# The mean of a group norm: token tiles added on GpSimd ahead of one matmul, with both halves of a convolution moved before it

## What is computed

```python
x = x + L0_conv(_ln_c(x))        # layer norm, in_proj, causal convolution of 4 taps, selective scan over 16 states, projection
t = t + L0_ffn(_ln_t(t))         # tokens; values rounded to fp8 ahead of a 256x256 linear layer
x = x + L1_conv(_ln_c(x))        # group norm with 32 groups, then attention over channels:
    # mean = jnp.mean(xg, axis=(2, 3, 4)); var = jnp.var(xg, axis=(2, 3, 4))
    # xn = (xg - mean) * rsqrt(var + EPS), then Q, K, V, softmax(Q K^T / 16), output linear layer
t = t + L1_ffn(_ln_t(t))         # mixture of 8 experts, the best 2 for each token
```

## Time and profile before

| what | value |
|---|---|
| median of 3 runs | 1844.05 us (1843.04 to 1844.74) |
| the profiled execution | 1846.15 us |
| its span, first to last instruction | 1844.4 us |
| mean granted TensorE clock | 0.960 |
| PE busy | 1562.0 us (85% of the span) |
| DVE busy | 1182.3 us (64%) |
| POOL busy | 1074.2 us (58%) |
| ACT busy | 946.9 us (51%) |

### The profile page before, as it was taken

One profiled execution on the slowest core, in us unless ns is written; L12 is line 12 of the kernel. 1 busy time (PEld: TensorE's weight loads), 2 busy tenths in 40 slices (PEclk: granted clock), 3 DMA queues, 4 the chain that ended last, 5 costly groups with the idle time before them and its releaser, 6 DMA issues. The chain is left out here.

```text
span 1844.4 us, 22487 instructions
## 1 busy us (share of the span) xinstructions
PE 1562.0 (85%) x6433; PEld 996.5 (54%) x6434; DVE 1182.3 (64%) x1368; ACT 946.9 (51%) x1758; POOL 1074.2 (58%) x574
## 2 busy tenths in 40 slices
PE   5588898988789888888898888773499999999997
PEld 2233335643335553333564333453388888888896
DVE  3399998489998579999658989846622222222222
ACT  6857665876664876775677666431022222222222
POOL 0499991279994159999037999400345555545543
PEclk9899999999999999999998999996699999999999
DMA  3256560156662057564025656552022222222221
GB/s 103 95 204 211 208 214 1 49 190 234 221 214 73 1 168 250 189 213 159 2 74 192 234 194 228 207 215 71 21 34 38 34 38 36 40 34 37 37 31 28
DMA packets 78400, 222.41 MB, mean 121 GB/s; under 512 B 12588, under 2 KB 31349, under 8 KB 74966
## 3 DMA queue, kind: packets, MB, share of 16 engines
q1 hardware_dynamic: 62390, 202.54, 31.6%
q0 software_dynamic: 15904, 18.66, 6.3%
HBM read 199.76 MB, written 19.82 MB: 119 GB/s over the span
## 5 line engine op out<-in xcount | busy, mean ns | idle before, releaser
L462 PE MATMUL psum<-HC_sb,ident_sb 128*128 128x512 f32 x768 | 371.4, 609 | 39.0 <-DVE HC_sb L1561 24.8
L462 PE MATMUL psum<-experts_sb 64*128 64x512 f32 (+5 forms) x882 | 275.3, 548 | 78.6 <-DVE HC_sb L1561 24.3
L1968 ACT ACTIVATE hgt_sb<-psum_moe,b_sb 128x256 f32<-128x256 f32 (+1 forms) x312 | 116.2, 455 | 380.8 <-PE psum_moe L1875 380.8
L1127 ACT ACTIVATE psum<-experts_sb 128x1024 f32<-128x1024 f32 x192 | 212.7, 1111 | 168.3 <-DVE experts_sb L1551 106.9
L1551 DVE TENSOR_TENSOR_SCAN experts_sb<-psum,DBX_sb 128x1024 f32<-128x1024 f32 x108 | 244.2, 2276 | 23.6 <-ACT psum L1127 17.2
L2120 DVE TENSOR_TENSOR YS_sb<-psum_moe,b_sb 128x256 f32<-128x256 f32 x71 | 30.2, 425 | 356.2 <-PE psum_moe L1875 356.2
L1875 PE MATMUL psum_moe<-XGT_sb,w1s_sb 128*128 128x256 f32 (+1 forms) x1248 | 254.1, 362 | 0.0
L1875 PE MATMUL psum_moe<-experts_sb,hgt_sb 128*128 x1136 | 251.7, 379 | 0.7 <-DVE YS_sb L2120 0.7
L1852 POOL DMA_INDIRECT out<-YS_sb,scat_sb x71 | 129.1, 1818 | 207.2 <-DVE YS_sb L2124 192.1
L462 PEld LDWEIGHTS psum<-HC_sb,ident_sb 128*128 128x128 f32 x768 | 139.4, 192 | 199.8 <-issue 101.7
L1875 PEld LDWEIGHTS psum_moe<-XGT_sb,w1s_sb 128*128 128x128 f32 x1248 | 219.0, 191 | 25.3
(11 more groups left out here) (298 smaller groups left out, 2379.4 us busy)
## 6 DMA issues: line engine op xcount, KB each, us to landing
DA_sb<-bc_rows SPq DMA_DIRECT2D x96, 512.0 KB, 4.8
X_XT_sb<-bc_rows SPq DMA_DIRECT2D x92, 512.0 KB, 4.1
experts_sb<-bc_rows SPq DMA_DIRECT2D x48, 512.0 KB, 5.1
SQ_sb<-bc_rows SPq DMA_DIRECT2D x48, 512.0 KB, 5.4
T_sb<-bc_rows SPq DMA_DIRECT2D x20, 512.0 KB, 5.8
experts_sb<-w1T SPq DMA_DIRECT2D x8, 1024.0 KB, 18.5
experts_sb<-w2T SPq DMA_DIRECT2D x8, 1024.0 KB, 20.4
X_sb<-x_tok SPq DMA_DIRECT2D x5, 1024.0 KB, 6.9
```

The source lines that it names most:

```text
L462: return nc.tensor.matmul(o, lhsT, rhs, start=start, stop=stop, **k)
L1127: nc.scalar.activation(DECAY_SB if is_turned(i) else decays[i % 2], DT[:, c, :], ACT.Exp, scale=a_neg[:, s:s + 1]).then_inc(da_ready, 1)
L1968: m = nc.scalar.activation(HGT[:, k, 4 * h + q, 0:w], psum[:, 2 * h + q // 2, (q % 2) * 2 * P:(q % 2) * 2 * P + w], ACT.Gelu, bias=b1[:, b ...
```

## The change

POOL adds the eight normed token tiles of an image into `HSUM`, 256 columns of `SQ`, with seven additions, each of which waits for its tile and for the addition before it (the first also for the end of the fp8 rounding, whose scratch lies there). PE then needs one matmul with `mean_w`. It waits for the seventh addition of the image, and in PE's list the second half of the convolution stands ahead of it. On POOL the additions come first in `between`; for the last image they follow after the loop.

```diff
+        HSUM = SQ[:, 0, HL + C:L]
...
             def group_sum(p):
-                for n in range(NB):
-                    pe.wait_ge(h_done, p * NB + n + 1)
-                    i = mm(psum[:, 0, 0:C], mean_w[:, :], XT[:, n, 0:C], n == 0, n == NB - 1)
-                i.then_inc(gm_ready, 1)
+                pe.wait_ge(token_sum, (p + 1) * (NB - 1))
+                mm(psum[:, 0, 0:C], mean_w[:, :], HSUM, True, True).then_inc(gm_ready, 1)
...
                 if go_on:
                     conv_pair(b, 1, 0)
+                    conv_pair(b, 1, 1)
                 group_sum(p)
-                if go_on:
-                    conv_pair(b, 1, 1)
                 gram(p)
...
+            def sum_tokens(p):
+                for n in range(1, NB):
+                    pool.wait_ge(h_done, p * NB + n + 1)
+                    if n == 1:
+                        pool.wait_ge(q_step, p * 10 + 10)
+                    else:
+                        pool.wait_ge(token_sum, p * (NB - 1) + (n - 1))
+                    nc.gpsimd.tensor_tensor(HSUM, HSUM if n > 1 else XT[:, 0, 0:C], XT[:, n, 0:C], ALU.add).then_inc(token_sum, 1)
+
             def between(b):
+                sum_tokens(b - 1)
                 pool.wait_ge(g_step, b * 5)
...
             with pool.Fori(1, B) as b:
                 between(b)
                 scans(b, True)
+            sum_tokens(B - 1)
```

More of the change, by code:

```diff
@@ L316, in build_front @@
         ff_ready = sem("ff_ready"); x2_done = sem("x2_done")
-        h_done = sem("h_done"); ones_set = sem("ones_set"); gm_ready = sem("gm_ready"); gm_done = sem("gm_done")
+        h_done = sem("h_done"); token_sum = sem("token_sum"); ones_set = sem("ones_set"); gm_ready = sem("gm_ready"); gm_done = sem("gm_done")
         hc_done = sem("hc_done"); gram_ready = sem("gram_ready"); gram_done = sem("gram_done")
```

## The result

The change made the kernel slower: a median of 1848.81 us (1847.70 to 1853.25, 7 runs) against 1843.04 us for the kernel before in the same comparison (1841.79 to 1844.74, 7 runs), a ratio of 1.0034 with a 95% interval of 1.0022 to 1.0045, so +6.3 us (+4.1 to +8.3). The profiled execution took 1849.37 us with a span of 1847.5 and a mean granted clock of 0.952; before it was 1846.15, 1844.4 and 0.960. The change shifted the helper's line from L462 to L464.

A forecast was written before the change was run, and what follows sets the result against it. PE sets the pace in conv stages; the last stage is one chain. Three times -0.2, plus 2.4, 0.5, 1.9 and 3.0, gave +7.2 us: 1851.2 on the 1844.05 median, range 1846.0 to 1855.5.

The forecast's parts named there:

- the leading case: Clock lost in the last stage and in two or three conv stages: 1849.5 to 1855.5 us, chance 0.57.
- the first rival: Clock lost in the last stage and in one conv stage at most: 1848.2 to 1849.8 us, chance 0.25.
- POOL's step: Start to start of POOL's chained adds at the norm: 0.87 us, bounds 0.73 and 0.96.
- The conv stages' term: Gram matrix in each of three conv stages starts 0.2 us earlier; bounds -0.9 to +0.4.
- The last stage's chain: Last stage: POOL's adds delay DVE's start on the mean by 2.4 us; bounds +1.6 and +3.0.
- The mean at half clock: Last stage: the one mean matmul runs at 1.2 GHz and takes twice as long, +0.5 us.
- The gram matrix of the last stage: Last stage: gram matrix at 1.2 GHz for its first 3.8 us, +1.9 us; bounds 0 and 7.2.
- The conv stages' clock: Two of three conv stages lose the full clock at 1.5 us each, +3.0 us; bounds none and three.
- The row before 590: Second stage, old profile: PE ran 1.43 of 3.5 us before 590; the next 3.5 stood at 0.52 clock.
- no clock is lost at all: Rival: full clock kept in all stages, +1.8 us, 1845.9 us, no measurable change; chance 0.14.
- The faster one: Rival: conv stages get back all 3.3 us of PE's work each, -7.5 us in sum, 1836.6 us; chance 0.04.
- the late mean in the last stage: Sign for the prediction: last stage, DVE starts on the mean 2.4 us or more later, counted from ACT's first normed tile.

The follow-up runs named there:

- e3: The whole change plus matmuls with unread results around the mean in the last stage, against the kernel before: 1844.50 us, ratio 1.0002.
- e6: The whole change plus matmuls with unread results after the mean in conv stages and around it in the last, against the kernel before: 1843.65 us, ratio 0.9997.
- e5: POOL's sum and one matmul, but in the old place between the convolution's halves, against the kernel before: 1854.71 us, ratio 1.0057.
- e9: The changed kernel run once more, unaltered, against the kernel before: 1848.24 us, ratio 1.0031.
- e4: Second half of the convolution moved ahead of the mean, which still takes eight matmuls, against the kernel before: 1852.92 us, ratio 1.0054.
- e2: The change in conv stages only, plus four matmuls with unread results behind the mean there, against the kernel before: 1840.92 us, ratio 0.9982.

## Why the prediction was right, and where its steps were not

The time, 1848.81, lies in the range, 2.4 us under the forecast, and the cause is the one that was forecast: POOL's chain in the last stage, and PE's clock where the tiles no longer keep it at work. But it lies below 1849.5, where the range of the leading case began, and inside the 1848.2 to 1849.8 of the first rival, and both traces of the change show that rival's one loss in a conv stage. Most terms of the sum were mis-sized, and their errors partly cancel; that the total came so near is in part luck.

**POOL's step** is the first: 0.87 us was taken. In the conv stage six adds in a row take 4.49 us, with 0.75 from start to start, near the lower bound of 0.73; in the last stage 4.79, with 0.81. POOL's timeline of the changed kernel, the first two of these six in either stage:

```profile
324.38 0.64 POOL L1210 TENSOR_TENSOR SQ_sb<-SQ_sb,X_XT_sb 128x256 f32<-128x256 f32 x1
325.09 0.73 POOL L1210 TENSOR_TENSOR SQ_sb<-SQ_sb,X_XT_sb 128x256 f32<-128x256 f32 x1
...
1206.80 0.64 POOL L1210 TENSOR_TENSOR SQ_sb<-SQ_sb,X_XT_sb 128x256 f32<-128x256 f32 x1
1207.58 0.72 POOL L1210 TENSOR_TENSOR SQ_sb<-SQ_sb,X_XT_sb 128x256 f32<-128x256 f32 x1
```

The adds last 0.64 to 0.73 us instead of 0.731, and the gap between dependent ones is 0.07 us in the conv stage and 0.14, as taken, in the last. From the second tile to the seventh add's end the conv stage took 328.87 - 323.43 = 5.44 us, the last 5.70, where 6.15 had been summed up. The rule of the Trainium skill (Perfetto Trace Analysis, section GPSIMD Engine Instruction) on spacing is borne out again: 0.75 and 0.81 from start to start beside a median span of 0.68.

**The conv stages' term** of -0.2 follows from it and was too small: -0.93, at the edge of its bounds. DVE starts on the mean 0.44 us later than before (7.26 us behind the first tile against 6.82), not 1.15, and the half microsecond that PE was to wait for the sum is all but absent. The weight load ahead of the mean stood idle for 0.78 us, put down to POOL; before, with nothing to wait for, it was 0.76:

```profile
324.06 3.33 PEld L462 LDWEIGHTS psum<-X_XT_sb,mean_w_sb 128*128 128x128 f32 x16 [0.76 <-issue]
```

**The last stage's chain**, +2.4, measured +1.98 (e3, e6): the short step again. **The mean at half clock**, +0.5, was right: 1.22 us against 0.70.

**The gram matrix of the last stage** was put at +1.9. It measured +3.04 in the change, +3.0 in e5 and +2.08 in e9. The direction and the mechanism hold; in the change the return took some 6.1 us of dense work (twice the 3.04 lost), and 4.2 in e9, where the middle of the two returns of the earlier trace rows had been 3.8.

**The conv stages' clock**, two losses of 1.5, is the step that was right on average and wrong in its argument. A loss costs 1.69 (the rows that gave 1.5 differ by 32.38 - 30.81 = 1.57). Over the four runs with this order and POOL's sum the clock fell in 6 of 12 stages (one, two, two and one), so 2.5 us a run instead of 3.0; both executions of the change itself show one loss, which is the case of the first rival. But the argument was the emptiness of a stretch, 0.5 us of PE between two idle times, and there is no such stretch: by the records PE works through the convolution and the mean without a gap. One idle time is left, 2.20 us, and e4, with 10.8 us of gapless work ahead of the same gap, lost the clock too. The row before 590 that the choice rested on was another case.

By the rule of the Trainium skill that stood with that rival (TensorE: Matmul & The Clock Gate, section HAM oscillation) the conv stages would all keep the clock. The runs disagree: behind a gap of 2.20 us it was lost in 7 of 15 conv stages (e4's among them). That a gap is what does it, the runs do bear out: with the gap cut to 0.47 us it was lost in none of 12.

**The rivals.** That no clock is lost at all is refuted by every trace of the changed order without idle matmuls; e6 is what it would have looked like, and there the change is worth nothing that can be measured. The faster one failed where it was said to: the mean comes 0.4 us later than before, so the centring never has the convolution beside it.

Of the signs named, the late mean in the last stage (2.48 us), the two microseconds of idle time behind the mean, and gram matrices over 8 us where the clock fell came true. Two signs against are there too: steps under 0.87, and, in the conv stages, a PE that doesn't wait for the sum. That part of the sum was wrong.

What stays open is why one stage loses the clock behind the same gap and the next doesn't, and how much of the 5.8 us between the medians is due to stretches away from the norm. The account of the 3.1 us above is of one execution of each kernel, and spans vary by several microseconds.

## What to carry to other kernels

A matmul that looks redundant may be what keeps PE at full clock. Before taking such work from PE, look at what idle time it leaves ahead of the next long stretch of matmuls; a few matmuls whose results nobody reads can fill it, if they delay nothing, and here four of them turned no gain into 3.3 us. A chain on a slower engine pays where other work covers it (the conv stages, 0.93 us gained in each) and costs its length where it stands alone (the last stage, 2.0), so make such an edit in the stages with cover only.

## What the hardware showed that was not expected

- The granted clock after a gap isn't the same from one execution to the next. Behind 2.20 us of idle PE it fell in 7 of 15 conv stages, in other stages in each execution; behind 0.47 in none of 12; behind 3.38 (e5) in all three.
- The return isn't constant either: the gram matrix of the last stage took 10.22, 10.19 and 9.26 us in three executions of the same instructions. The Trainium skill (TensorE: Matmul & The Clock Gate, section Part 1: The HAM clock gate) says of the slow matmuls at the start of a kernel that their number is "run-variable"; the returns here, behind a fall within the kernel, vary too.
- The kernel before varies with it: 1840.80 to 1849.69 us in 29 runs of one comparison, where its first three runs had shown 1.7 us between them. The difference of 3.3 us in e2 took twelve runs of it to show.
- POOL's dependent adds of 128x256 last from 0.63 to 0.73 us with the same shape, and follow each other within 0.07 us in the conv stage but 0.14 in the last, where the transfers ran at a share of 1.01 beside them (0.00 in the conv stage); whether these are the cause wasn't tried.
